# Sparse expert tiles routed through DRAM, stage by stage, in place of dense experts woven with the sampling convolution

## The chip, the core and the metric

One core of a Trainium2 chip runs one program. The metric is device time in microseconds. TensorE multiplies matrices (PE in the profile, PEld for its weight loads), VectorE is DVE, ScalarE is ACT, GpSimd is POOL, and SyncE (SP) issues most of the DMAs.

## The reference, cut to what matters

A batch of 8 images of 64 channels and 16x16 pixels goes through four residual blocks. A token is a pixel; there are 256 per image and 2048 in all.

```python
x = x + conv(ln_c(x))      # deformable sampling: 8 groups x 9 taps, bilinear, offsets from a depthwise conv; 2 products; SiLU
t = t + ffn0(ln_t(t))      # 8 experts, hidden 682: sum_e gates[n,e] * (silu(x w1_e) * (x w3_e)) w2_e ; gates: top 2 of 8
x = x + attention(ln_c(x)) # linear attention, 8 heads of 32: softmax(q), softmax(k), context = k v^T
t = t + ffn1(ln_t(t))      # 16 experts, hidden 128, same form, top 2 of 16
```

The reference computes every expert for every token and multiplies by gates, all but two of which are zero.

## The kernel before

Work is done image by image. The program has two streams of steps. `stream_a` of an image holds its layer norm, values, depthwise convolution, offsets, the sampling taps, the first residual and the routing of the first expert block. `stream_b` holds the experts of that block, attention, the second routing and the experts of the last block. A first walk does `stream_a` of image 0 while the expert weights are split into high and low parts (`piece`, L833). A loop of 7 rounds then weaves `stream_a` of image i with `stream_b` of image i-1, and a final walk does `stream_b` of image 7 alone. The order on each engine is written out by hand in `WEAVE`. Engines wait for each other through semaphores.

**Sampling.** A sampled value is a sum over 16 columns (a matrix product) and 16 rows (an elementwise product and a later sum). `columns` makes column distances on TensorE (L439, 2 groups of 128 partitions per tap), ScalarE turns them into weights (L693, L695), and `column_weights` stores them as high and low parts in `hx` (L898, L900). A unit is one tap k, one token tile t of 128 and one half h of the groups: two products of 512 columns (`bdh` L453, `bdl` L454), a multiplication by the row weights `hy` on VectorE out of PSUM (L914), and an addition into `acc` on GpSimd (L1084). There are 36 units per image, with two PSUM banks and two `prod` buffers. `hy` is made by L890 (DVE), L683, L687 (ACT) and L1075 (POOL). L921 sums the rows at the end.

**Experts.** Both blocks are dense: every expert runs over all 256 tokens of the image. A pair is two chunks of up to 128 hidden rows. `up` makes eight products of 256 columns (L523, L524, L537, L538), ScalarE applies SiLU (L752), VectorE multiplies (L985), and `down` adds two products into one bank (L548). There are 24 pairs for block 0 and 8 for block 1 in each image. The gate is applied beforehand: `gated` (L738, 4 scalings on ScalarE per two experts) makes a scaled copy of the input, `gate_unit` transposes (L503) and splits it (L745, L978). All weights stay in SBUF.

**Routing.** `top` finds the two largest logits, `gates` makes a row of gates for each token.

Layer norms take their inverse root on GpSimd (L1068, L1070).

Of the kernel before, what the change touches and what calls it, by code (L numbers as in the profile page):

```python
# [8 lines left out]
TT = PIX // P  # L29
G, GC, K = 8, 8, 9  # L30
GH = 4
NH = G // GH
E0, HID0, CH0 = 8, 682, 114
CPE0 = -(-HID0 // CH0)
E1, CH1 = 16, 128
NC0, NC1 = E0 * CPE0, E1
PAIRS0, PAIRS1 = NC0 // 2, NC1 // 2
PAIRS = PAIRS0 + PAIRS1
PPE0 = CPE0 // 2
UNITS = K * TT * NH  # L40
ADDS = UNITS - TT * NH
GU0, GU1 = E0 // 2, E1 // 2
SLOTS = 4
# [3 lines left out]
AUG = C + 4  # L47
STAGE = 1024
LAG = 2
RING = 6  # L50


def gating(m, first, end):

    out = []
    for u in range(first, end):
        out += [("gated", m, u)] + ([("gate_unit", m, u - 1)] if u > first else [])
    return out + [("gate_unit", m, end - 1)]

WEAVE = {
    "pe": """
        bbabbbbabb bbbbbabbbb bbbababbba bbbbbbbbbb bbbbabbaba abbaababba bbabaaaaba bababababa aabbabbaaa abaabaaaaa
        abaabaabbb abaabaabab bbabaababa bbabbbbbab ababa
        """,
    "act": """
        bbbabbbbab bbbbaabbba abbaabbaba bbbbbaabab bbbababbba bbabbbbbbb bbbbbbbbaa babbabaabb baaaaabaaa
        """,
    "dve": """  # L70
        babbabbbba bbaabababb baabbbbbba aaababbaab aabbaabaaa abbaaaabba baababaaba baabaabaaa aaabaabbab abababaaab
        bababaabab aabbababaa
        """,
    "pool": """
        aaaaabaaaa aaaaaaabaa aaaaaaaaaa aaaaaaaa
        """,
}


def stream_a():  # L80

    pre = [("x_tokens",), ("stats", 0), ("norm", 0), ("xn_channels",), ("cv1",), ("y",), ("values",)]
    pre += [("depthwise", r) for r in range(3)] + [("diagonal",), ("offsets",)]
    pre += [("row_distances", t) for t in range(TT)] + [("row_weights", t) for t in range(TT)]

    taps = [("columns", 0), ("column_weights", 0), ("columns", 1)]
    for k in range(K):
        units = [("tap" if k else "first_tap", k, q) for q in range(TT * NH)]
        taps += units[:1] + ([("column_weights", k + 1)] if k + 1 < K else [])
        taps += units[1:2] + ([("columns", k + 2)] if k + 2 < K else []) + units[2:]  # L90
    tail = [("sampled",), ("op",), ("cv2",), ("x1",), ("stats", 1), ("norm", 1), ("stack", 0), ("logits", 0), ("top", 0),
            ("exp", 0), ("gates", 0)]
    return pre + taps + tail + gating(0, 0, GU0)


def stream_b():

    def pairs(first, end, late=()):
        out = []
        for j in range(first, end):  # L100
            out += [("up", j)]
            out += (late[j - first] if j - first < len(late) else []) + ([("down", j - LAG)] if j >= first + LAG else [])
        return out + [("down", j) for j in range(end - LAG, end)]
    att = [("x2",), ("x2_tokens",), ("stats", 2), ("norm", 2), ("xn2_channels",), ("queries",), ("keys",),
           ("attn_values",), ("k_maxima",), ("q_maxima",), ("k_exp",), ("v_copy",), ("q_exp",), ("k_tokens",), ("context",),
           ("q_norm",), ("q_channels",), ("mix",), ("attend",), ("x3_tokens",), ("stats", 3), ("norm", 3), ("stack", 1),
           ("logits", 1), ("top", 1), ("exp", 1), ("gates", 1)]
    att += gating(1, 0, SLOTS)
# [42 lines left out]
def count(x):  # L151

    if isinstance(x, int):
        return x
# [1000 lines left out]
```

## Time and profile before

| | |
|---|---|
| runs, us | 1307.42, 1313.4, 1317.43; median 1313.4 |
| profiled execution, first to last instruction | 1318.4 us |
| PE, DVE, ACT, POOL busy | 1045.0, 849.9, 592.8, 395.3 us |
| mean granted TensorE clock | 0.813 of 2.4 GHz |
| DMA | 12.32 MB, mean 9 GB/s |

The profiled execution's own device time is not listed apart from its span. The span lies 0.4% above the median of the runs and inside 0.1% of the slowest of them, so nothing of size lies around it. Busy shares are averages over the first walk, seven rounds and the final walk.

### The profile page before, as it was taken

How to read it: one execution, taken by the hardware profiler on the slowest of the kernel's cores; microseconds unless marked ns; L12 is line 12 of the kernel's file. 1: busy time of each engine (PE TensorE's matmuls, PEld its weight loads, DVE VectorE, ACT ScalarE, POOL GpSimd, SP SyncE). 2: the span in 40 equal slices, each digit the busy share in tenths (PEclk: the TensorE clock that was granted, in tenths of full speed). 3: DMA queues.
4: the chain of work that ended last, by engine and by line, in shares of the span. 5: the costliest groups of instructions: out<-in, count | busy, mean ns of one | idle time of the engine just before them, and what ended most of it. 6: DMA issues, size and time to landing. Idle time of an engine off the chain costs nothing.

```text
span 1318.4 us, 17175 instructions
## 1 busy us (share of the span) xinstructions
PE 1045.0 (79%) x5184; PEld 712.9 (54%) x5184; DVE 849.9 (64%) x1608; ACT 592.8 (45%) x1261; POOL 395.3 (30%) x340
## 2 busy tenths in 40 slices
PE   2574697779887898778977798678976898779856
PEld 1341574546654675555745465455744575456534
DVE  2786567955587456964679556974688456974332
ACT  1422543563435634455435634455435624366343
POOL 0275015610265004630156103640157002650000
PEclk9955788778987778778887798888988779878956
DMA  4122000000000000000000000000000000000000
GB/s 129 53 67 66 19 1 1 1 3 3 0 0 0 5 0 0 0 2 3 0 0 0 4 1 0 0 2 3 0 0 0 4 0 0 0 0 3 0 1 2
DMA packets 5326, 12.32 MB, mean 9 GB/s; under 512 B 1118, under 2 KB 2342, under 8 KB 5094
## 3 DMA queue, kind: packets, MB, share of 16 engines
q1 hardware_dynamic: 4782, 9.02, 2.6%
q10 hardware_dynamic: 494, 2.81, 0.7%
q14 instruction: 40, 0.33, 0.1%
q8 instruction: 10, 0.16, 0.1%
HBM read 11.30 MB, written 0.52 MB: 9 GB/s over the span
## 4 chain that ended last, share of the span: by engine, by line
PE 54%; DVE 18%; issue 11%; ACT 8%; POOL 6%; DMA 1%; DVEq 0%; POOLq 0%; SPq 0%; ACTq 0%
PE ps_y L548 11%; PE ps_h L523 7%; POOL sb_acc L1084 5%; PE ps_h L537 5%; PE ps_h L524 4%; PE ps_h L538 4%; PE ps_t L453 4%; ACT sb_xg L738 4%; DVE sb_prod L914 3%; PE ps_m L439 3%; PE ps_t L454 3%; PE ps_t L421 3%; PE ps_h L503 2%; DVE sb_hx L898 2%; DVE sb_dsum L921 1%
## 5 line engine op out<-in xcount | busy, mean ns | idle before, releaser
L1084 POOL TENSOR_TENSOR sb_acc<-sb_acc,sb_prod 128x512 f32<-128x512 f32 x256 | 332.7, 1322 | 231.9 <-DVE sb_prod L914 230.6
L752 ACT ACTIVATE sb_hid<-ps_h 114x512 f32<-114x512 f32 (+1 forms) x256 | 149.8, 595 | 245.5 <-PE ps_h L524 245.0
L985 DVE TENSOR_TENSOR sb_hid<-ps_h,sb_hid 114x512 f32<-114x512 f32 (+1 forms) x256 | 171.8, 685 | 136.7 <-ACT sb_hid L752 104.0
L453 PE MATMUL ps_t<-sb_bdh,sb_hx 128*128 128x512 f32 x288 | 165.6, 575 | 62.8 <-DVE sb_prod L914 58.8
L914 DVE TENSOR_TENSOR sb_prod<-ps_t,sb_hy 128x512 f32<-128x512 f32 x256 | 172.1, 684 | 32.0 <-PE ps_t L454 17.1
L454 PE MATMUL ps_t<-sb_bdl,sb_hx 128*128 128x512 f32 x288 | 137.9, 479 | 0.0
L453 PEld LDWEIGHTS ps_t<-sb_bdh,sb_hx 128*128 128x128 f32 x288 | 66.5, 231 | 130.9 <-DVE sb_prod L914 103.4
L548 PE MATMUL ps_y<-sb_hid,sb_w2s 114*64 114x256 f32 x768 | 131.4, 426 | 0.0
L738 ACT ACTIVATE sb_xg<-sb_xn,sb_gt 128x128 f32<-128x128 f32 x384 | 120.1, 390 | 25.0 <-DVE sb_gt L973 25.0
L523 PE MATMUL ps_h<-sb_xh,sb_w1s 128*114 128x256 f32 x384 | 125.0, 345 | 0.0
L1068 POOL TENSOR_TENSOR sb_rs<-sb_mv,sb_epst 128x2 f32<-128x2 f32 x32 | 6.2, 195 | 375.1 <-DVE sb_mv L846 375.1
L537 PE MATMUL ps_h<-sb_xgh,sb_w3s 128*114 128x256 f32 x384 | 107.9, 300 | 9.6 <-DVE sb_hid L985 9.6
L1075 POOL TENSOR_TENSOR sb_hy<-sb_hy,sb_ym 128x1152 f32<-128x1152 f32 x16 | 34.2, 2155 | 263.4 <-ACT sb_hy L687 263.4
L439 PE MATMUL ps_m<-sb_dwT,sb_omx 68*128 68x256 f32 x288 | 99.8, 480 | 15.2 <-ACT sb_hat L693 13.8
L538 PE MATMUL ps_h<-sb_xgl,sb_w3s 128*114 128x256 f32 x384 | 106.6, 297 | 0.0
L524 PE MATMUL ps_h<-sb_xl,sb_w1s 128*114 128x256 f32 x384 | 106.0, 296 | 0.0
L523 PEld LDWEIGHTS ps_h<-sb_xh,sb_w1s 128*114 128x114 f32 x384 | 73.5, 191 | 57.2 <-ACT sb_hid L752 31.2
L693 ACT ACTIVATE sb_hat<-ps_m 128x512 f32<-128x512 f32 x72 | 42.8, 594 | 133.6 <-DVE sb_hx L900 127.3
L900 DVE SCALAR_TENSOR_TENSOR sb_hx<-sb_hx,sb_wide,sb_hat 128x512 fp32r<-128x512 f32 x72 | 96.7, 1343 | 2.5
L439 PEld LDWEIGHTS ps_m<-sb_dwT,sb_omx 68*128 68x128 f32 x288 | 65.9, 243 | 36.9 <-ACT sb_hat L693 17.7
L537 PEld LDWEIGHTS ps_h<-sb_xgh,sb_w3s 128*114 128x114 f32 x384 | 74.0, 193 | 11.3 <-DVE sb_hid L985 11.3
L524 PEld LDWEIGHTS ps_h<-sb_xl,sb_w1s 128*114 128x114 f32 x384 | 74.4, 194 | 1.4
(173 smaller groups left out, 1794.4 us busy)
## 6 DMA issues: line engine op xcount, KB each, us to landing
sb_hid<-in_w1T SPq DMA_DIRECT2D x16, 171.0 KB, 3.1
sb_hid<-in_w3T SPq DMA_DIRECT2D x16, 171.0 KB, 3.0
sb_w2s<-in_w2T ACTq DMA_DIRECT2D x1, 1368.0 KB
sb_hid<-in_u1T SPq DMA_DIRECT2D x4, 256.0 KB, 3.9
sb_hid<-in_u2T SPq DMA_DIRECT2D x4, 256.0 KB, 3.7
sb_omx<-in_omxT ACTq DMA_DIRECT2D x1, 612.0 KB
sb_xT<-in_x SPq DMA_DIRECT2D x8, 64.0 KB, 2.1
sb_u3s<-in_u3T ACTq DMA_DIRECT2D x1, 512.0 KB
```

Source lines behind the costliest of these rows:

```text
L439: last = mm(mb[:, h * PIX:(h + 1) * PIX], omx[:, o:o + P], dwT[:, :], start=True, stop=True)
L453: mm(tb[u % 2][:, :], w, bdh[:, h, :], start=True, stop=False)
L454: mm(tb[u % 2][:, :], w, bdl[:, h, :], start=False, stop=True).then_inc(s_pe_t, 1)
L523: mm(d, wa[:, o:o + ch], xh[m][:, :], start=True, stop=False)
L524: last = mm(d, wa[:, o:o + ch], xl[m][:, :], start=False, stop=True)
L537: mm(d, wb[:, o:o + ch], xgh[m][:, slot, x], start=True, stop=False)
L538: last = mm(d, wb[:, o:o + ch], xgl[m][:, slot, x], start=False, stop=True)
L548: last = mm(yb[c * C:(c + 1) * C, 0:PIX], w[0:ch, 2 * (j - first) + c, :], hid[0:ch, j % RING, c * PIX:(c + 1) * PIX], start=(j == first), ...
L738: last = af(xg[m][:, u % 2, t, e, :], xn[1 + 2 * m][:, t, :], ACT.Copy, scale=gt[m][:, t, 2 * u + e:2 * u + e + 1])
L914: v.tensor_tensor(o.rearrange("p (g c q) -> p g c q", g=GH, q=H), tb[u % 2][:, :].rearrange("p (g c q) -> p g c q", g=GH, q=H), w, ALU.mul ...
L985: v.tensor_tensor(hid[0:ch, j % RING, :], h3[j % 2][0:ch, :], hid[0:ch, j % RING, :], ALU.mult).then_inc(s_dve_hid, 1)
L1084: g.tensor_tensor(acc[:, t, h, :], acc[:, t, h, :], prod[:, u % 2, :], ALU.add).then_inc(s_pool_acc, 1)
```

## The change

The whole batch now goes through the blocks one after the other: `conv_order`, `moe0_order`, `attention_order`, `moe1_order`, `final_order`. Everything is unrolled; a step takes its place by a number, and an image's steps before and after its taps are spread over the taps of its neighbours.

**Sampling.** A unit is one tap and one token tile with all eight groups: four single products of 256 columns (K is 2 groups x 16 columns x 2 parts of the column weights x 2 parts of the values), 1024 elements for VectorE and for GpSimd. There are 18 units per image and three `prod` buffers. The column weights of three taps are made at once (128 x 768): ScalarE takes absolute value, ReLU and a high part, VectorE the low part, and SP copies these with 16 DMAs (32 partitions x 3 KB each) into the four partition groups of `hx`. The depthwise convolution is 9 products on TensorE, the second multiplication of `rows` is on VectorE, and the two output products become one (`opcv`).

**Experts.** Ranks of tokens within their experts are counted with products (`upper`, `ones`). `scatter` writes each normalized token to two rows of `xs` in DRAM. `route` makes tables of tiles on VectorE. Block 0 then runs 23 tiles (J0) of 256 rows with one expert each, 3 pairs per tile; block 1 runs 32 tiles (J1), two at a time. SP reads expert and row from the tables into registers and loads rows and weights of each tile from DRAM. Results go to `ys`; `gather` fetches two rows per token, and the gates are applied to them.

```diff
+        xs = nc.dram_tensor("xs", (E1 * CAP, C), f32).ap()
+        ys = nc.dram_tensor("ys", (J1 * TILE, C), f32).ap()
+            for g in range(E1):
+                sp.dma_start(xs[g * CAP:(g + 1) * CAP, :].rearrange("(p r) c -> p (r c)", p=P), zero[:, :]).then_inc(s_zero, 16)
...
+            def columns(n, r):                                     # SP
+                sp.wait_ge(s_act_hh, 2 * q + 2)
+                for part, src in ((0, hath[b]), (2, hath[b]), (1, hatl[b]), (3, hatl[b])):
+                    if part == 1:
+                        sp.wait_ge(s_dve_hl, q + 1)
+                    for j in range(NJ):
+                        sp.dma_start(hx[s][32 * part:32 * part + 32, j, :].bitcast(f32),
+                                     src[32 * j:32 * j + 32, :].bitcast(f32)).then_inc(s_hx[s], 16)
...
+            def load0(j):                                          # SP
+                e = sp.value_load(tab[0][0:1, 0, j:j + 1], min_val=0, max_val=E0 - 1)
+                r = sp.value_load(tab[0][0:1, 1, j:j + 1], min_val=0, max_val=E0 * CAP - TILE)
+                if j >= 2:
+                    sp.wait_ge(s_pe_mx, j - 1)
+                for d in range(2):
+                    sp.dma_start(xt[b][:, :, d, :], rows).then_inc(s_ldx[b], 16)
+                if j >= 2:
+                    sp.wait_ge(s_pe_dn, PAIRS * (j - 1))
+                sp.dma_start(w13[b][:, :].bitcast(f32), wsp[:, bass.ds(e * (2 * W0), 2 * W0)]).then_inc(s_ldw[b], 16)
+                sp.dma_start(w2[b][:, :], A["w2T"][:, bass.ds(e * (CPE0 * C), CPE0 * C)]).then_inc(s_ldw[b], 16)
...
+            def tap(n, k, t):                                      # TensorE
+                for j in range(NJ):
+                    last = mm(tb[u % 2][:, j * 256:(j + 1) * 256], hx[q % 3][:, j, o:o + P], vbd[n % 2][:, j * 256:(j + 1) * 256],
+                              start=True, stop=True)
...
+            def scatter(n, m):                                     # GpSimd
+                for t in range(TT):
+                    for z in range(2):
+                        g.indirect_dma_start(out=xs, out_offset=bass.IndirectOffsetOnAxis(ap=idx[m][:, TT * n + t, z:z + 1], axis=0),
+                                             in_=xr[m][n % 2][:, t, :], in_offset=None).then_inc(s_sc[m][n % 2], 16)
+            def gather(n, m):                                      # GpSimd
+                for t in range(TT):
+                    for z in range(2):
+                        g.indirect_dma_start(out=yg[b][:, t, z, :], out_offset=None, in_=ys[0:NJT[m] * TILE, :],
+                                             in_offset=bass.IndirectOffsetOnAxis(ap=jdx[m][:, TT * n + t, z:z + 1], axis=0))
```

`load1` (block 1, two tiles) makes four register reads and eight DMAs in the same way: four of rows (64 KB each), two of `u12` (128 KB), two of `u3` (32 KB). `split_out` writes the split weights of both blocks to `wsp` and `usp` in DRAM.

## Rows read from the trace of the kernel before

**Rows 1.** The page's first part: engine, busy us and share, instructions.

```profile
PE 1045.0 (79%) x5184; PEld 712.9 (54%) x5184; DVE 849.9 (64%) x1608; ACT 592.8 (45%) x1261; POOL 395.3 (30%) x340
```

**Rows 2.** The page's chain of waits, its shares by engine.

```profile
PE 54%; DVE 18%; issue 11%; ACT 8%; POOL 6%; DMA 1%; DVEq 0%; POOLq 0%; SPq 0%; ACTq 0%
```

**Rows 3.** The timeline of SP's queue: image loads of two successive rounds.

```profile
274.90 0.49 SPq L376 DMA_DIRECT2D sb_xT<-in_x  x1
...
428.53 0.49 SPq L376 DMA_DIRECT2D sb_xT<-in_x  x1
```

**Rows 4.** Busy time by window: stretch, length, busy of PE, PEld, DVE, ACT, POOL, clock, DMA.

```profile
0.00:19.60 19.60, 0.00 (x0) 0.00 (x0) 1.28 (x7) 0.00 (x0) 0.20 (x4) 1.00 0.59 153
60.00:118.00 58.00, 38.83 (x78) 22.00 (x78) 47.42 (x54) 14.12 (x22) 42.15 (x31) 0.54 0.25 68
200.00:360.00 160.00, 134.01 (x676) 91.31 (x675) 106.22 (x204) 74.42 (x159) 50.32 (x43) 0.83 0.01 1
1203.50:1244.50 41.00, 41.00 (x292) 28.73 (x292) 17.90 (x26) 15.36 (x26) 0.00 (x0) 1.00 0.01 3
1244.50:1276.50 32.00, 15.30 (x49) 10.54 (x48) 11.53 (x44) 7.23 (x20) 1.76 (x4) 0.57 0.00 1
1276.50:1318.40 41.90, 29.07 (x128) 20.40 (x128) 11.91 (x19) 20.40 (x50) 0.00 (x0) 0.62 0.01 2
```

**Rows 5.** Groups of instructions: busy us, mean ns; idle before and its releaser.

```profile
L914 DVE TENSOR_TENSOR sb_prod<-ps_t,sb_hy 128x512 f32<-128x512 f32 x256 | 172.1, 684 | 32.0 <-PE ps_t L454 17.1 <-POOL sb_acc L1084 13.5
...
L738 ACT ACTIVATE sb_xg<-sb_xn,sb_gt 128x128 f32<-128x128 f32 x384 | 120.1, 390 | 25.0 <-DVE sb_gt L973 25.0
L752 ACT ACTIVATE sb_hid<-ps_h 114x512 f32<-114x512 f32 x192 | 112.3, 594 | 182.1 <-PE ps_h L524 181.8
...
L439 PE MATMUL ps_m<-sb_dwT,sb_omx 68*128 68x256 f32 x288 | 99.8, 480 | 15.2 <-ACT sb_hat L693 13.8 <-ACT sb_ym L679 1.4
...
L1075 POOL TENSOR_TENSOR sb_hy<-sb_hy,sb_ym 128x1152 f32<-128x1152 f32 x16 | 34.2, 2155 | 263.4 <-ACT sb_hy L687 263.4
...
L1070 POOL TENSOR_TENSOR sb_rs<-sb_rs,sb_mhalf 128x2 f32<-128x2 f32 x32 | 22.3, 697 | 2.5
...
L890 DVE TENSOR_TENSOR sb_hy<-sb_ym,sb_wide 128x1152 f32<-128x1152 f32 x16 | 20.9, 1350 | 0.0
...
L921 DVE TENSOR_REDUCE sb_dsum<-sb_acc 128x64 f32<-128x1024 f32 x16 | 18.7, 1209 | 1.7 <-POOL sb_acc L1084 1.7
...
L886 DVE TENSOR_TENSOR sb_bdl<-sb_acc,sb_bdh 128x1024 fp32r<-128x1024 f32 x8 | 9.8, 1226 | 11.3 <-ACT sb_bdh L675 11.3
...
L1068 POOL TENSOR_TENSOR sb_rs<-sb_mv,sb_epst 128x2 f32<-128x2 f32 x32 | 6.2, 195 | 375.1 <-DVE sb_mv L846 375.1
```

**Rows 6.** Single lines: durations in ns as min/median/max, first and last start.

```profile
L1084 POOL TENSOR_TENSOR sb_acc<-sb_acc,sb_prod x256: 1257/1281/1906, 58.6 to 1173.7; 128x512 f32<-128x512 f32 x128
```
```profile
L900 DVE SCALAR_TENSOR_TENSOR sb_hx<-sb_hx,sb_wide,sb_hat x72: 750/1634/1654, 50.1 to 1162.5; 128x512 fp32r<-128x512 f32 x72
```
```profile
L833 DVE SCALAR_TENSOR_TENSOR sb_w1s<-sb_xgh,sb_wide,sb_hid x8: 916/925/2167, 26.7 to 68.9; 128x684 fp32r<-128x684 f32 x8
```
```profile
L371 SPq DMA_DIRECT2D sb_hid<-in_w1T x16: 465/597/828, 3.1 to 58.4; - x16
```

**Rows 7.** DMA queue, and issues with KB each and median us to landing.

```profile
q1 hardware_dynamic: 4782, 9.02, 2.6%
```
```profile
sb_hid<-in_w1T SPq DMA_DIRECT2D x16, 171.0 KB, 3.1
...
sb_xT<-in_x SPq DMA_DIRECT2D x8, 64.0 KB, 2.1
```

More of the change, by code:

```diff
@@ L47, with spread, conv_order @@
 AUG = C + 4
+UNITS = K * TT
+ADDS = UNITS - TT
+TRI = 3
+NTRI = K // TRI
+RING = 4
+W0 = CPE0 * CH0
 STAGE = 1024
-LAG = 2
-RING = 6
-def gating(m, first, end):
+def spread(steps, start, end):
+    return [(start + (end - start) * (i + 0.5) / len(steps), s) for i, s in enumerate(steps)]
+def conv_order(n_pieces):
     out = []
[L56 to L77, printed above, removed]
@@ L80, in stream_a @@
[L80 to L93, printed above, removed]
@@ L96, in stream_b @@
[L96 to L108, printed above, removed]
-    late = [[]] + [[("gated", 1, u), ("gate_unit", 1, u)] for u in range(SLOTS, GU1)]
-    return pairs(0, PAIRS0) + att + pairs(PAIRS0, PAIRS, late) + [("x4",)]
@@ L644, in _ @@
+            pe.wait_ge(s_const, n_const)
+            pe.wait_ge(s_set, 4)
+            mm(pb[0:C, 0:C], op_[:, :], cv2[:, :], start=True, stop=True).then_inc(s_pe_comb, 1)
+            for name, *args in order:
+                if name in steps:
+                    steps[name](*args)
         @block.scalar
@@ L797, in walk @@
[L797 to L805 removed]
+                    af(ex[m][:, t, :], lg[m][:, t, :], ACT.Exp, bias=nm[m][:, t:t + 1], accum_out=sm[m][:, t:t + 1])
@@ L808, in _ @@
+            for name, *args in order:
+                if name in steps:
+                    steps[name](*args)
         @block.vector
@@ L1047, in walk @@
-            def walk(order, images):
-                for stream, name, *args in order:
-                    if name in steps:
-                        steps[name](images[stream], *args)
-            walk(first, {"a": 0, "w": 0})
-            with dve.Fori(1, B) as i:
-                walk(steady_order(WEAVE["dve"], steps), {"a": Image(i, 0), "b": Image(i, -1)})
-            walk(final, {"b": B - 1})
+                b = n % 2
+                dve.wait_ge(s_pe_mm, n + 1)
+                dve.wait_ge(s_dve_qn, 5 * n + 5)
@@ L1058, in _ @@
+            for name, *args in order:
+                if name in steps:
+                    steps[name](*args)
         @block.gpsimd
@@ L1086, in _ @@
-            steps = {"stats": rsqrt, "row_weights": row_weights, "tap": tap}
-            def walk(order, images):
-                for stream, name, *args in order:
-                    if name in steps:
-                        steps[name](images[stream], *args)
-            walk(first, {"a": 0, "w": 0})
-            with pool.Fori(1, B) as i:
-                walk(steady_order(WEAVE["pool"], steps), {"a": Image(i, 0), "b": Image(i, -1)})
-            walk(final, {"b": B - 1})
+            pool.wait_ge(s_set, 4)
@@ new lines, in stats0, with stats1, combine, stats3 @@
+            def stats0(n):
+                rsqrt(n, 0)
+            def stats1(n):
+                rsqrt(n, 1)
+            def combine(n):
+                rsqrt(n, 2)
+            def stats3(n):
+                rsqrt(n, 3)
+            steps = {"stats0": stats0, "stats1": stats1, "combine": combine, "stats3": stats3, "tap": tap, "scatter": scatter, "mout": mout, "gather": gather, "nout": nout}
+            for name, *args in order:
+                if name in steps:
+                    steps[name](*args)
```

1629 lines of the change are left out of this document (968 added, 661 removed).

## The prediction

> **What bounds the kernel now.** Read the busy shares first [rows 1]: TensorE has 79% of the span, VectorE 64%, and no engine is full. The chain of waits [rows 2] gives TensorE 54% and VectorE 18%, so the end is set by TensorE work and by handovers. The windows [rows 4] split that. In a round (200 to 360) TensorE is busy 134 of 160 us at a clock of 0.83, VectorE 106. The rounds follow each other at 153.6 us (274.90 to 428.53 [rows 3]). The final walk shows what `stream_b` costs alone: 41.0 us for the 24 pairs of block 0, with TensorE full at clock 1.00 (2.4 GHz), or 1.71 us per pair; 32.0 us for attention and the second routing, a bare chain in which TensorE is busy 15.3 us at 0.57, near the lower level of 1.2 GHz; and 41.9 us for block 1. So dense experts are about a third to a half of the work, sampling most of the rest. The first walk (60 to 118) shows sampling without experts: GpSimd busy 42.15 of 58 us, VectorE 47.42, and TensorE at 0.54 is not the limit. That stretch matters most, because the change makes sampling a stage of its own.
>
> **The change, part by part.** The sum is made against the span of 1318.4 us and scaled by 1313.4/1318.4 at the end. Stages no longer overlap, so their times add.
>
> *Start.* TensorE begins at 19.6 us today, when the constants have landed [rows 4]. After, 16 fills of 512 KB (8.4 MB) stand on SP's queue before the first copies into `hx`. SP's queue moved 9.02 MB in 2.6% of 16 engines' 1318.4 us, 548 engine-us, so 263 GB/s with all 16 busy [rows 7]. The fills take 32 us, constants and images before them 5 to 10, and the copies another few: the first tap at 48 us. If the fills were free it would be about 42, at half the rate 75.
>
> *Sampling, per image.* Four parts:
> - TensorE halves its columns, from 72 x 512 to 72 x 256. It was not the limit in the first walk and gains nothing here.
> - GpSimd adds 16 x 1024 elements. No row has this shape. Half the elements take 1257 ns at least [rows 6], 1152 elements of another product 2155 [rows 5]. Twice the first is 2.51 us, the line through both shapes gives 1.98. I take 2.32, twice 1257 less the 195 ns that a two-element addition costs [rows 5], since that keeps the same operation: 37.1 us.
> - VectorE's taps go from 36 x 0.684 to 18 x 1.22 us (1024 elements at L886's 1226 [rows 5]), 22 us. Operations with two SBUF inputs are three low parts of 768 elements (0.95 each by the same rows), four of 1152 for the row weights (1.35), one of 1024 (1.28), and the split of weights, 20 pieces over 8 images (2.5 us an image at 916 ns for 684 elements [rows 6]): 12.1 us. Sums of rows are 2 x 1.21. With layer norms, top-2 and ranks, some 7 us of small ones, VectorE has about 43.
> - L900 takes 750 ns alone and 1634 in the median, while GpSimd's addition goes from 1257 to 1906 [rows 6]. The two seem to exclude each other. So the additions and the 12.1 us are added: 49.2. GpSimd also has two inverse roots (0.9 each) and four indirect DMAs for the scatter, 5.2 us, in all 56.2.
>
> In the first walk's stretch GpSimd's busy time and the free-standing durations of VectorE's two-input work fill nearly all 58 us; I divide by 0.96: 58.5. Three places drain the ring. At the image border no addition runs while VectorE sums rows and multiplies twice (5 us), since tap 0 has no addition. At each of two layer norms VectorE waits for GpSimd and then restarts it (2.2 us each). That gives 68 us per image, 544 for 8. The bounds are 58 (no drain visible) and 75.
>
> The Trainium skill (SBUF — State Buffer, Who interferes with whom) says that VectorE with two SBUF inputs and GpSimd reading SBUF exclude each other for whole instructions. The trace agrees, 750 against 1634 ns. Without that rule an image would cost the larger of 43 and 44 plus drains, about 54, and the sum would be 112 us lower; with it, the 1024-wide addition holds VectorE off for up to 2.3 us at a time.
>
> *Indirect DMAs* (32 for each of two scatters and two gathers). No row shows one. Nearest below is SP's issue, 0.53 us, above it GpSimd's 2.16 us instruction [rows 5, 6]. I take 1.3 of GpSimd's time each, the middle, and 2.1 us to landing as for the small load [rows 7].
>
> *From the last tap to the first expert product.* Nothing overlaps: sums, two products, SiLU, residual, norm, logits, top-2, ranks are 20 to 23 us by the 32 us chain of attention, whose second half holds the same steps. Four scatters, landing, two register reads and the first 0.9 MB of weights add 18. I take 41.
>
> *Block 0.* 69 pairs stand in place of 192. A tile is 3 x 1.71 + 0.6 us for its transposes, 5.7 at full clock. Its weights (896 KB) may load only when the tile two before is done. From issue to landing that is 0.5 + 3.4 (896 KB at 263 GB/s) + 1.9 = 5.8 us. A buffer is in use 6.0 us at 2.4 GHz, 7.2 at the rounds' 0.83. Two buffers give (7.2 + 5.8)/2 = 6.5 us per tile, 150 for 23. Bounds: 125 (TensorE alone) and 220 (clock at its lower level, as in the 0.54 stretch). The gating (L738's 120 us of ScalarE) goes; it was beside other work but not in the final walk.
>
> *Attention.* Into it 13 us (last tile out, gather, landing). The lone chain was 32.0 us; ranks make it 35. Two images are in flight, 17.5 each if they matched. GpSimd must issue 8 indirect DMAs (10.4 us) and their landing between one image's ranks and the next combination but one, where some 7 us are free: 5 us more. I take 23 each, 8 x 23 + 15 = 199. Bounds are 150 and 255. The clock will be low: the same steps ran at 0.57.
>
> *Block 1.* Into it 18 us, as before block 0. TensorE needs about 2.8 us per two tiles at 2.4 GHz, 5 at 1.2. SP issues 8 DMAs at 0.53 and makes 4 register reads from SBUF. No row has a register read; it lies between nothing and the 2.1 us of a small load's landing. I take 0.8, near the issue. 4.2 + 3.2 = 7.4 us, so SP is the bound: 16 x 7.4 = 118. Bounds are 80 and 200.
>
> *End.* Store landing 3, 32 gathers at 1.3 = 42, last tokens out 7: 52.
>
> **Sum:** 48 + 544 + 41 + 150 + 13 + 199 + 18 + 118 + 52 = 1183 us; times 0.9962 is 1178.
>
> **Rivals.**
> *Handovers hide better.* Sampling at 58 an image (-80), attention at 18 (-40), block 0 at 125 (-25), block 1 at 80 (-38): 1000. For it: VectorE and GpSimd have three buffers now, not two. Against: in no window of before did an engine stay full but TensorE in the pure expert walk.
>
> *Indirect DMAs cost GpSimd 2.2 us, not 1.3.* Sampling +29, attention +58, end +29, transitions +11: 1310, scaled 1305. It becomes no change at that price. Nothing in the trace speaks against it, as GpSimd issues no DMA at all now. The Trainium skill (DMA: Bandwidth & Descriptors, Specifications) gives GpSimd's path about 1 us to the first byte; by it the sum would be some 30 us lower. No run here shows it.
>
> *The copies into `hx` set the pace (slower than before).* Three taps' weights are ordered five of six units ahead, 5 x 68/18 = 18.9 us. The way there is three products (L439), three ScalarE passes of some 0.85 us by L752's 594 for 512, a low part (0.95), together 5.6 us, then 16 issues on SP's queue and 2.1 to land [rows 5, 7]. At 0.53 us an issue this is 16.2, just hidden. From 0.70 us it decides, and at 1.2, with 8.0 us of stall in each of 24 triples, it gives 1183 + 192, scaled 1370. L371 takes 465 to 828 ns [rows 6], so the threshold lies inside the spread that one line shows; but its median is 597, and SP had little else. SP also issues each split's three DMAs in that order.
>
> That the change doesn't cut the work is excluded: J0 and J1 are fixed tile counts, and 69 pairs and 32 tiles are issued whatever the routing.
>
> **How the numbers follow.** The forecast as summed has 0.48, with its own range of 1070 to 1270. The fast rival has 0.18, costly indirect DMAs 0.18, the copies 0.16. A measurement of this kernel tells about 1% from no change, so 1300 to 1327 is "same". The forecast and the fast case are faster, the indirect case is split between faster (0.09) and same or worse, the copies are slower. Faster 0.76, same 0.07, slower 0.17. The range leaves out half of the fast case's low side and most of the copies' case beyond 1370: 990 to 1370. Of single terms the sampling stage carries the widest money, 8 x (58 to 75).
>
> **What the profile after would show.** Right: five stages in the slices; in sampling, GpSimd busy two thirds or more with additions near 2.3 us, VectorE's low parts stretched beyond 0.95, little waiting for `hx`; block 0 at 6 to 7 us per tile with TensorE waiting for weight DMAs; attention at 23 us an image, clock near 0.5; SP's queue dense in block 1. Wrong: TensorE waiting in sampling for `hx` (copies), GpSimd's queue filled by indirect DMAs, additions of 2.0 us or of more than 2.6, or a clock at 1.2 GHz through block 0.

## The result and the profile after

The changed kernel takes 1373.2 us (median of 4, 1369.0 to 1374.5) against 1310.5 for the kernel before beside it: a ratio of 1.047, 95% interval 1.042 to 1.052. It is slower. The forecast was 1178 us and faster, with a range up to 1370, so the sign was wrong. The profiled execution has a span of 1370.3 us.

The page's first part, as [rows 1] of before:

```profile
PE 749.1 (55%) x3080; PEld 556.4 (41%) x3080; DVE 603.9 (44%) x1158; ACT 331.9 (24%) x605; POOL 518.1 (38%) x379
```

Every engine but GpSimd lost work, TensorE 296 us and VectorE 246. No engine now has more than 55% of a longer span, so the time was lost in waits. That GpSimd is busy 51% of the sampling stage, where the forecast named two thirds or more as the sign of being right, is the first hint. The windows cut at the stages (columns as in [rows 4]; start, sampling, tail and routing, block 0, attention, routing, block 1, end) say where:

```profile
0.00:56.00 56.00, 21.44 (x68) 14.66 (x68) 14.74 (x37) 14.63 (x18) 1.10 (x6) 1.00 0.58 203
56.00:762.00 706.00, 372.50 (x1274) 285.29 (x1274) 381.39 (x475) 182.25 (x264) 362.81 (x184) 0.92 0.30 75
762.00:790.00 28.00, 6.41 (x22) 3.94 (x22) 11.04 (x50) 7.06 (x15) 4.82 (x6) 0.50 0.15 44
790.00:956.00 166.00, 143.13 (x964) 101.91 (x964) 63.80 (x114) 58.49 (x114) 16.37 (x23) 0.94 0.49 146
956.00:1203.00 247.00, 128.33 (x448) 102.78 (x448) 92.72 (x393) 41.57 (x137) 78.84 (x96) 0.50 0.04 9
1203.00:1211.00 8.00, 0.00 (x0) 0.00 (x0) 3.44 (x11) 0.00 (x0) 0.96 (x1) 0.50 0.18 42
1211.00:1318.00 107.00, 71.38 (x286) 46.08 (x286) 28.51 (x47) 24.50 (x48) 20.24 (x29) 0.60 0.40 104
1318.00:1370.30 52.30, 5.90 (x20) 1.76 (x18) 8.27 (x33) 3.40 (x9) 32.92 (x36) 0.50 0.16 35
```

Against the forecast: start 56 (48), sampling 706 (544), tail 28 (41), block 0 166 (150), attention with the way into it 247 (212), routing 8 (18), block 1 107 (118), end 52.3 (52). Sampling is off by 162 us and attention by 35; the rest cancels. In sampling VectorE and GpSimd are each busy about half of the time. The waits of that stretch, by engine and releaser (total us, times, longest us):

```profile
POOL sb_acc L1310 <- DVE sb_prod L1044: 366.5, 72, 63.5
DVE sb_stage_w L983 <- ACT sb_stage_h L761: 101.3, 15, 14.1
DVE sb_hats L1030 <- ACT sb_hats L814: 55.0, 22, 3.9
ACT sb_stage_h L761 <- DMA sb_stage<-in_w1T: 49.4, 7, 13.9
ACT sb_stage_h L761 <- DMA sb_stage<-in_w3T: 47.8, 6, 14.3
DVE sb_prod L1044 <- PE ps_t L504: 35.5, 28, 6.3
DVE sb_hy L1022 <- ACT sb_hy L800: 33.9, 14, 2.4
DVE sb_vbd L1011 <- ACT sb_vh L783: 33.5, 7, 6.0
DVE sb_xn L997 <- POOL sb_rs L1362: 20.0, 7, 2.9
```

L1030 makes the low part of the column weights, L1022 is the last multiplication of the row weights, L1011 lays out the values for the products, L997 is the last operation of a layer norm.

Read it from the top. GpSimd, whose additions were to be the larger part of the bound, waits 366 us for VectorE's products, 63.5 of them before its first addition. Between its first addition and its last (80.8 to 761.1 us) GpSimd is idle for 317 us. In 187 of them VectorE works, 96 on products of taps and 91 on its other instructions; in the other 131 both stand. VectorE's own waits are mostly within its steps, for ScalarE or GpSimd to do the middle of them. The largest in total is at the split of the weights (L983), and ScalarE in turn waits there for a load.

The spacing of the row sums (L1052) gives the time of an image. They start at 165.0, 268.4, 371.5, 463.3, 544.3, 625.4, 704.0 and 761.1 us: 103 us for images 1 and 2, with five weight pieces in each spacing, 92 for image 3 with four, 81.1 for images 4 and 5 without pieces, 78.6 for image 6, which took 81.1 in the other kernels with the same sampling, and 57 for the last, which prepares no successor. The forecast had 68 for all.

### The profile page after: what moved, and what is told of

Its sections match the earlier page's. It is cut to its first block and busy times, and to the rows that moved or that the text cites. A ratio compares the mean times of both kernels' runs of the same rounds, so it can differ in the third digit from the quotient of the medians.

```text
span 1370.3 us, 10821 instructions
## 1 busy us (share of the span) xinstructions
PE 749.1 (55%) x3080; PEld 556.4 (41%) x3080; DVE 603.9 (44%) x1158; ACT 331.9 (24%) x605; POOL 518.1 (38%) x379
## 5 line engine op out<-in xcount | busy, mean ns | idle before, releaser
L1310 POOL TENSOR_TENSOR sb_acc<-sb_acc,sb_prod 128x1024 f32<-128x1024 f32 x128 | 307.3, 2417 | 366.6 <-DVE sb_prod L1044 366.5
L504 PE MATMUL ps_t<-sb_vbd,sb_hx 128*128 128x256 f32 x576 | 171.6, 454 | 179.8 <-DVE sb_prod L1044 148.0
L504 PEld LDWEIGHTS ps_t<-sb_vbd,sb_hx 128*128 128x128 f32 x576 | 134.7, 321 | 216.9 <-DVE sb_prod L1044 161.5
L1044 DVE TENSOR_TENSOR sb_prod<-ps_t,sb_hy 128x1024 f32<-128x1024 f32 x128 | 153.5, 1218 | 43.8 <-PE ps_t L504 35.5
L1322 POOL DMA_INDIRECT xs<-sb_xr,sb_idx x64 | 81.7, 1276 | 105.1 <-DVE sb_idx L1121 89.3
L983 DVE SCALAR_TENSOR_TENSOR sb_stage_w<-sb_stage_h,sb_wide,sb_stage 128x684 fp32r<-128x684 f32 (+1 forms) x20 | 27.4, 1372 | 101.3 <-ACT sb_stage_h L761 101.3
L1345 POOL DMA_INDIRECT sb_prod<-ys,sb_jdx x64 | 61.3, 958 | 23.0 <-issue 20.9
L1030 DVE TENSOR_TENSOR sb_hats<-sb_hat,sb_hats 128x768 fp32r<-128x768 f32 x24 | 36.6, 1526 | 66.2 <-ACT sb_hats L814 66.2
L490 PE MATMUL ps_c<-sb_dwT,sb_omx 68*128 68x256 f32 x144 | 65.0, 623 | 0.0
L474 PE MATMUL ps_pa<-sb_ypad,sb_diag 64*64 64x256 f32 x144 | 63.5, 634 | 0.0
L865 ACT ACTIVATE sb_stage<-ps_t 114x512 f32<-114x512 f32 x69 | 41.2, 597 | 70.3 <-PE ps_t L572 68.5
L468 PE MATMUL ps_c<-sb_vp,sb_yrep 65*128 65x64 f32 x256 | 53.9, 409 | 2.5 <-ACT sb_yrep L771 2.4
L468 PEld LDWEIGHTS ps_c<-sb_vp,sb_yrep 65*128 65x128 f32 x256 | 53.3, 321 | 3.6 <-ACT sb_yrep L771 3.2
L571 PE MATMUL ps_t<-sb_hx,sb_hats 128*114 128x256 f32 x138 | 44.2, 340 | 12.2 <-DMA sb_acc<-in_w2T 11.7
L1022 DVE TENSOR_TENSOR sb_hy<-sb_hy,sb_ym 128x1152 f32<-128x1152 f32 x16 | 30.6, 1911 | 38.8 <-ACT sb_hy L800 38.8
```

The lines of the kernel that those rows point to most:

```text
L468: last = mm(cb[:, r * C:(r + 1) * C], yrep[:, r * P:(r + 1) * P], vp[:, :], start=True, stop=True)
L474: last = mm(pa[0:C, 0:PIX], diag[:, k, :], ypad[:, k // 3:k // 3 + H, k % 3:k % 3 + W], start=(k == 0), stop=(k == K - 1))
L490: last = mm(cb[:, i * PIX:(i + 1) * PIX], omx[:, k * P:(k + 1) * P], dwT[n % 2][:, :], start=True, stop=True)
L504: last = mm(tb[u % 2][:, j * 256:(j + 1) * 256], hx[q % 3][:, j, o:o + P], vbd[n % 2][:, j * 256:(j + 1) * 256], start=True, stop=True)
L571: mm(d, w13[b][:, o:o + CH0], xh[b][:, :], start=True, stop=False)
L865: af(hid[q % RING][0:CH0, :], h1[q % 2][0:CH0, :], ACT.Silu).then_inc(s_act_s, 1)
```

## The experiments

Two theories of the stage. *O, order:* VectorE runs its steps in program order, and the middle of a step on another engine leaves it standing while GpSimd has nothing to add. *X, exclusion:* GpSimd's additions and VectorE's instructions with SBUF operands alone can't run together, and their sum is the bound. Beside them stood *C*, the rival of the prediction, the copies into `hx`. For attention: *G*, a chain through GpSimd's order, against *K*, TensorE's low clock and the hops.

The medians (us), each with the kernel before on the same chip; "image" is the spacing of row sums of an image without pieces, "last sum" the start of the last pair of row sums in the profile:

```
kernel                            time    before   ratio (95%)             image  last sum
changed                           1373.2  1310.5   1.047 (1.042-1.052)     81.1   761.1
loads early                       1317.5  1310.0   1.005 (1.001-1.010)     81.1   705.6
no split                          1286.5  1310.0   0.982 (0.973-0.991)     81.1   673.6
VectorE in two phases             1307.7  1310.0   1.001 (0.997-1.004)     75.7   696.9
no additions                      1310.1  1310.0   0.998 (0.995-1.001)     72.2   699.1
gathers ahead                     1333.0  1317.3   1.014 (1.005-1.022)     81.1   764.1
loads early and two phases        1299.3  1317.3   0.988 (0.979-0.998)     75.8   687.6
three engines, gathers ahead      1231.7  1317.3   0.937 (0.928-0.945)     72.0   662.5
half copies                       1378.5  1317.3   1.048 (1.039-1.057)     81.0   767.3
chain later, combine ahead        1207.6  1310.2   0.924 (0.919-0.930)     74.4   650.1
units of 512                      1352.5  1310.2   1.034 (1.027-1.041)     76.3   737.7
all orders, units of 512          1200.6  1312.0   0.912 (0.905-0.919)     70.3   643.5
three engines, no additions       1159.1  1312.0   0.881 (0.871-0.890)     64.4   587.8
```

The kernel before took 1310.0, 1317.3, 1310.2 and 1312.0 us beside them, on four chips. So where rows of different chips lie within some 10 us of each other, their ratios are to be compared, not their times. Four kernels leave work out and only price it: no split (the weights stay unsplit), the two without additions, and half copies.

### The pieces of weights

Loads early:

```diff
+    out += [(0.05 + 0.2 * i - 0.12, ("piece_high", i)) for i in range(n_pieces)]
 # SP, in piece(j), behind the write of piece j - 1:
-                load(j)
+                load(j + 1)
 # ScalarE takes its part at piece_high, VectorE at piece
```

> Each piece's two loads are issued one piece earlier (on SP, behind the write of the piece before), and ScalarE makes its high part 0.12 of an image ahead of VectorE's low part; nothing else moves. Theory O (order: VectorE, whose program order holds the low part, the hats, the rows and the additions' products, stands in a wait while GpSimd has nothing to add): the 20 low parts of L983 waited 101 + 15 + 14 us in all, and most of that goes: sampling 706 -> 610 to 640 us, the total 1373 -> about 1290, all of it in images 0 to 3 (103 -> 84 us each). Rival C (SP's queue of 16 copies for each group of three taps sets the pace): the same transfers stand in the same queue, so at most 10 to 20 us go. Rival X (GpSimd's additions and VectorE's SBUF-only instructions can't run at the same time, and their sum is the bound): 20 low parts of 1.3 us each remain in the sum, so 103 stays near 95, total about 1340.

Measured: 56 us less. Images 1 and 2 take 87 and 90 us instead of 103, image 3 90. L983's wait has left the head of VectorE's list. Sampling ends 56 us earlier where O had named 66 to 96; C had at most 20 and X some 33 for the total, so O is nearest, and too high.

No split:

```diff
-            steps = {"piece": piece, ...          (ScalarE and VectorE)
 # SP: wsp and usp are written from stage as it was loaded
```

> The split of the weights into a high and a low part is left out: the pieces are loaded and written back as they are, and neither ScalarE nor VectorE touches them (so the products of block 0 and block 1 take unsplit weights; times of these stages are the same). It prices all that the pieces cost the two engines. Theory O: images 0 to 3 take what images 4 to 6 take, 81 us instead of 103: total 1373 - 90 = about 1283, and close to the run with the loads issued earlier (within 30 us of it). Rival C: the 60 transfers of the pieces remain, so under 30 us go. Rival X: 20 x 1.3 us of SBUF-only work go, with their waits remaining elsewhere: about 1340.

Measured: 87 us less, and all images from 1 to 6 take 81.1 us. So the pieces cost 87 us in all, of which the late loads, with ScalarE's part standing directly before VectorE's, were 56. The forecast had charged VectorE's own time for them, 2.5 us an image, 20 in all. The 31 us that stay with early loads are close to the 27.4 us for which L983 is busy in the changed kernel (20 instances, 921 to 3177 ns: some are held by additions).

### VectorE in two phases

```diff
+LATE = ("rows", "columns", "values", "stats0", "stats1", "top", "piece")
+    out += [(t + 0.07, (s[0] + "_late", *s[1:])) for t, s in out if s[0] in LATE]
 # VectorE, in rows: the subtraction stays at "rows",
 # the wait for ScalarE and the multiplication stand at "rows_late", the others alike
```

> VectorE's second halves, those that wait for ScalarE, GpSimd or SP within a step (rows' multiplication, the low part of the hats, the values' block form, the norms' last operation, the gates, the low part of a piece), stand 0.07 of an image (one or two taps) later in VectorE's order; the other engines' orders stay, and no work is added or removed. Theory O: of VectorE's 325 us of idle time in sampling the waits inside steps (of the order of 250 us with the pieces') are filled with taps: images 4 to 6 fall from 81 to 62-68 us, images 0 to 3 from 103 to 75-85; total about 1220 to 1260. Rival X: GpSimd's 16 additions (37.6 us) and VectorE's SBUF-only instructions (some 18 us) follow one another, with 8 us of GpSimd's other work: not under 64 us an image, and likely 72; total about 1300. Rival L (the chain of ten steps that prepares the next image sets the period, through ScalarE and TensorE): the late halves lengthen this chain, so the time stays or grows: 1370 to 1420.

Measured: 66 us less, an image 81.1 -> 75.7. L falls. The direction is O's, but it had named 113 to 153 us in all and 13 to 19 an image. The total of about 1300 was X's figure, so this run alone doesn't part O from X; the next does. Windows of one image without pieces, of the changed kernel first, then of this one:

```profile
546.60:627.70 81.10, 50.20 (x170) 38.40 (x170) 46.90 (x63) 23.09 (x34) 47.15 (x24) 1.00 0.26 61
```

```profile
488.30:564.00 75.70, 50.14 (x170) 38.24 (x170) 53.02 (x63) 23.21 (x34) 47.74 (x24) 1.00 0.27 63
```

VectorE idles 22.7 us instead of 34.2, but the same 63 instructions take 6.1 us longer: more of them now meet an addition. The largest part is the two last operations of a layer norm, in the changed kernel and in this one:

```profile
562.80 0.54 DVE L997 TENSOR_SCALAR sb_xr<-sb_x1t,sb_mv,sb_rs 128x64 f32<-128x64 f32 x2 [2.86 <-POOL sb_rs L1362]
```

```profile
502.33 4.63 DVE L1003 TENSOR_SCALAR sb_xr<-sb_x1t,sb_mv,sb_rs 128x64 f32<-128x64 f32 x2
```

What is left of the waits in this image is mostly for TensorE:

```profile
DVE sb_prod L1057 <- PE ps_t L506: 16.0, 6, 6.7
DVE sb_dsum L1065 <- POOL sb_acc L1330: 2.3, 1, 2.3
```

TensorE issues 16 and 9 products of the next image in one go, and it stands in its own order for the sums and norms of the image before.

### No additions

```diff
-g.tensor_tensor(acc[n % 2][:, t, :], acc[n % 2][:, t, :], prod[a % 3][:, :], ALU.add)
+g.tensor_tensor(acc[n % 2][:, t, 0:8], acc[n % 2][:, t, 0:8], prod[a % 3][:, 0:8], ALU.add)
```

> GpSimd adds 8 columns of the 1024 of each tap instead of all (so the sampled sums lack the rest); everything else, the waits too, stays. Theory O: GpSimd isn't the bound, it is starved: only the instructions of VectorE that were held to the end of an addition, and the taps that found the ring full (8 us), get shorter: 6 to 12 us an image, total 1373 - 50 to 100 = 1275 to 1325, and an image without pieces takes 70 us or more. Rival X (GpSimd's additions, alone or with VectorE's SBUF-only work, are the bound): an image without pieces falls to VectorE's 45 to 50 us, total about 1100.

Measured: 63 us less, an image 72.2. GpSimd is busy 10.8 us of it. So GpSimd's additions are no bound (X in its strong form falls: it said 45 to 50), but they cost 9 us an image by what they do to VectorE. The row weights' multiplication (L1022), durations in ns as min/median/max, with the additions and without:

```profile
L1022 DVE TENSOR_TENSOR sb_hy<-sb_hy,sb_ym x16: 1357/1359/4305, 49.3 to 690.0; 128x1152 f32<-128x1152 f32 x16
L1077 DVE TENSOR_SCALAR sb_nm<-sb_mx x16: 168/170/2264, 208.9 to 1194.8; 128x2 f32<-128x2 f32 x16
```

```profile
L1022 DVE TENSOR_TENSOR sb_hy<-sb_hy,sb_ym x16: 1357/1359/1368, 49.5 to 647.7; 128x1152 f32<-128x1152 f32 x16
L1077 DVE TENSOR_SCALAR sb_nm<-sb_mx x16: 168/169/170, 206.2 to 1131.8; 128x2 f32<-128x2 f32 x16
```

Without additions no instance is stretched. An image has VectorE busy 37.9 us instead of 46.9, and that 9.0 us is the whole gain of 8.9. The product of a tap, which reads PSUM, isn't held at all:

```profile
L1044 DVE TENSOR_TENSOR sb_prod<-ps_t,sb_hy x128: 1206/1217/1226, 79.5 to 754.3; 128x1024 f32<-128x1024 f32 x128
L1310 POOL TENSOR_TENSOR sb_acc<-sb_acc,sb_prod x128: 2327/2352/3473, 80.8 to 758.8; 128x1024 f32<-128x1024 f32 x128
```

### The copies

```diff
-sp.dma_start(hx[s][32 * part:32 * part + 32, j, :], src[32 * j:32 * j + 32, :])
+sp.dma_start(hx[s][32 * part:32 * part + 32, j, 0:384], src[32 * j:32 * j + 32, 0:384])
```

> Each of the 384 copies into the taps' operand takes half of the 768 columns (the other half is zeroed once, so its taps are left out of the sums); the number of transfers stays. Theory O: the first copy alone had TensorE waiting, so the time stays within 15 us of 1373. Rival C (the copies' transfer time sets the pace of the taps): an image takes 8 us less or more, total about 1300.

Measured: 1378.5, a ratio of 1.048 against the changed kernel's 1.047: no difference. The copies' transfer time costs nothing. Their number was not varied; that it costs little too rests on the changed kernel's trace, where TensorE waits for a copy once:

```profile
  PE ps_t L504: 14.4, 1
```

### Both edits of VectorE's order, then TensorE's order too

> Both edits of sampling together: the pieces' loads one piece earlier with ScalarE ahead of VectorE (alone it gave 56 us), and VectorE's second halves 0.07 of an image later (alone 66 us, in which VectorE still waited 64 us for pieces). If both are waits of VectorE's order, they add up in most: images 0 to 3 fall to 80, images 4 to 6 stay at 75.7: total 1265 to 1285. If TensorE's order is by now what holds the period (in the two-phase run VectorE waited 16 of 75.7 us for it), the sum is less: images 0 to 3 stay at 85 or more, total 1290 to 1300.

Measured: 1299.3. By the ratios to the kernel before, that is some 17 us better than two phases alone and 23 better than early loads alone, where the two had given 66 and 56. The gains don't add: images 1 to 3 stay at 89 to 91 us. That is the second of the two expectations: in this kernel VectorE waits 93.5 us for TensorE's products between 100 and 640 us, about as in the run with two phases alone (89.7 us). That images with pieces gain so little is not explained further.

```diff
+# TensorE: values in 8 + 8 products, depthwise in 3 + 3 + 3, taps between them
+        out += [(n - 0.6, ("values_first", n)), (n - 0.52, ("depthwise_first", n, 0)),
+                (n - 0.47, ("depthwise_first", n, 1)), (n - 0.41, ("depthwise", n)), (n - 0.355, ("offsets", n))]
-        out += spread([("sampled", n), ("z", n), ("x1", n), ...], n + 1.02, n + 1.75)
+        out += [(n + 1.1, ("sampled", n)), (n + 1.16, ("sampled_next", n)), (n + 1.215, ("z", n)), ...]
+# "_next" is the place of TensorE's and ScalarE's part
```

> The edits of the two runs before, and also TensorE's side of sampling: the 16 products of the values and the 9 of the depthwise step stand in two and three parts between taps, and of the chain that follows the taps (sums, z, x1, norm, logits, ranks) each engine's step stands one tap behind that of the engine that it waits for; with the gathers ahead in attention. No work is added. Theory O, now for two engines: an image of sampling falls from 75.7 to 64-70 us (TensorE busy 50, VectorE 53, GpSimd 48), in all 8 images, sampling 706 -> about 570, attention to about 165: total 1373 - 136 - 80 = about 1155, between 1130 and 1200. Rival X (VectorE's SBUF-only work and the additions exclude one another, 9 us of an image by the run without additions): more overlap lengthens VectorE further, an image stays at 72 to 76: total about 1200 to 1230.

Measured: 1231.7 us, 6.3% faster than the kernel before. An image falls to 72.0 and the total to 1231.7. The first is the low end of X's 72 to 76, the second just past its 1200 to 1230; neither is in O's 64 to 70 and 1130 to 1200. X's mechanism is not seen, though: VectorE is busy 53.7 of 72.0, against 53.0 in the two-phase run, so there is hardly any further lengthening:

```profile
462.80:534.80 72.00, 50.75 (x172) 37.86 (x171) 53.74 (x63) 23.32 (x34) 47.02 (x24) 1.00 0.29 69
```

### What holds the rest

> The kernel of the run with three engines and the gathers, with GpSimd adding 8 columns of 1024 (the sampled sums lack the rest). In the changed kernel this took 9 us off an image of 81, all of it time by which VectorE's SBUF-only instructions had been held. With the waits inside VectorE's steps gone, theory X' (the additions and the holding are by now the larger part of what is above TensorE's 50 us) gives an image of 72 -> 58 to 62 us: total 1232 - 85 = about 1145. Rival P' (TensorE's order and VectorE's wait for its products, 14 to 16 us an image, is the larger part): 72 -> 64 to 67, total 1170 to 1185.

Measured: an image takes 64.4 us, a gain of 7.6 of 72.0 by the additions; P' named 64 to 67, and for the total 1170 to 1185. Measured were 1159.1, between that and the 1145 of X'. VectorE's busy time is 37.8. Between 100 and 600 us it waits, above all, for this:

```profile
DVE sb_prod L1074 <- PE ps_t L523: 174.3, 53, 14.7
```

So nearly without additions the stage would still take 14 us an image more than TensorE's 50.

> One part of the change alone is undone: the changed kernel's taps are taken in two units of 512 columns (products' release, VectorE's multiplication, GpSimd's addition, with the waits between them per half), all else as changed. Theory O: the size of the unit isn't what is slow; the halves cost VectorE 36 x 0.15 us/2 and GpSimd 0.16 us a tap more, under 3 us an image each, and a held instruction of VectorE waits for half as long: total 1373 within -20 and +25 us. Rival U (the large unit, with 2 in PSUM and 3 in the ring in place of finer ones, is what starves GpSimd): an image of 81 us falls to 72 or less: total 1300 or less.

```diff
 # tap(n, k, t), on TensorE, VectorE and GpSimd:
+for h in range(2):
+    c = slice(512 * h, 512 * h + 512)
     ... the same operation on [:, c], with a release and a wait of its own
```

Measured: 1352.5, 21 us less than the changed kernel (1.034 against 1.047 in the ratio), at the edge of what O allowed. The halves cost GpSimd 2.6 us of busy time an image more, and the image still takes 76.3 instead of 81.1. VectorE's busy time falls from 46.9 to 43.6: it is held for shorter additions (the small operation that took up to 2.26 us behind one now takes at most 1.09). The large unit was thus a loss of its own here, of about a third of the 63 us by which the change was slower.

> From the run with three engines' orders and the gathers, two further moves of order. In sampling the chain behind the taps (sums to scatter) stands 0.35 of an image later, out of the stretch in which TensorE also prepares the next image. In attention the combine step with its norm stands ahead of the ranks of the image two before (0.5n - 0.1 instead of + 0.075). Theory P (TensorE's crowded stretch, in which VectorE waited 14 of 72 us an image for its products, is what is left beside the exclusion): an image 72 -> 64 to 68 us, images with pieces 86 -> 78 to 82, sampling -35 to -50 us; attention's period 23.0 -> 18 to 20 us, -25 us; total 1232 -> 1155 to 1175. Rival X (GpSimd and VectorE exclude one another on SBUF operands, and a fuller overlap lengthens VectorE's instructions in its place): an image stays at 70 to 73 us, VectorE's busy time rises over 55 us; total about 1200. Rival K for attention (TensorE's 15 us of busy time at the clock of 0.50 and its order): the period stays at 21 to 23 us.

```diff
-out += [(n + 1.1, ("sampled", n)), ... (n + 1.76, ("scatter", n, 0))]
+out += [(n + 1.45, ("sampled", n)), ... (n + 2.11, ("scatter", n, 0))]
+out += [(0.5 * n - 0.1, ("combine", n))]      # attention, was at 0.5 * n + 0.075
```

Measured: 1207.6. P falls: an image takes 74.4 us, not 64 to 68. X's reading doesn't hold either, as VectorE's busy time falls to 49.7. Moving the chain out of the crowded stretch puts TensorE's waits elsewhere (39 us for the norm, 34 for the top-2, 25 for the next image's norm between 90 and 600 us). Still the stage ends 12 us earlier. The row sums stand a third of an image later here, so their spacings cover other pieces; counted from first tap to first tap, images 1 to 3 take 79, 80 and 83 us where they took 86, 86 and 89, a gain of 18, and images 4 to 6 lose 7. Why the images with pieces gain from the move stays open. Attention's period falls to 21.6, in K's range of 21 to 23 and not in the 18 to 20 of the other reading.

> The orders of the run with three engines (the chain behind the taps at its place there, not 0.35 later), the gathers and the combine step ahead in attention, and the taps in units of 512 columns as in the run that undid the units alone. If the units' gain (4.8 us an image there: 81.1 to 76.3) comes from shorter holds and waits between the three engines, it remains in part beside the mended orders: an image 72 -> 67 to 70 us, sampling -15 to -35 us against the run with three engines, attention 21.6 us an image: total 1180 to 1200. If the units' gain was the same waits that the orders have since removed, an image stays at 72 or rises by the 2.6 us of GpSimd's extra time: total 1205 to 1230.

Measured: 1200.6 us, 8.8% faster than the kernel before and the best of those that leave nothing out. An image takes 70.3 us, 0.3 above the first theory's range: 1.7 of the 4.8 us of the smaller unit remain beside the mended orders, so most of that gain was the same waits. Sampling ends 19 us before that of the run with three engines.

### Attention

In the changed kernel one image follows another at 30.2 us (first scatters at 1059.76 and 1089.94). The chain of waits between them, start, length, what (those through GpSimd):

```profile
1058.87 0.14 DVE sb_pick L1116
...
1059.76 1.06 POOL xs L1322
...
1063.66 1.44 POOL xs L1322
...
1065.40 1.00 POOL sb_prod L1345
...
1067.97 0.95 POOL sb_prod L1345
...
1069.23 2.37 DMA sb_prod<-ys,sb_jdx
1071.60 0.02 issue
1071.62 0.49 DVE sb_x2b L1181 x2
```

From the ranks of image n-2 to the combination of image n lie four scatters, four gathers and their landing, 11.8 us. The gathers depend on nothing in that chain; only GpSimd's order puts them behind.

```diff
-        out += spread([("gather", n, 0), ("combine", n), ...
+        out += [(0.5 * n - 0.26, ("gather", n, 0))]
```

> In the attention stage the four gathers of image n stand ahead of the four scatters of image n-2 in GpSimd's order (at 0.5n - 0.26 instead of 0.5n + 0.025); no work is changed. Theory G (the period of 30.2 us an image is a chain through GpSimd's order: rank, 4 scatters 5.3 us, 4 gathers 5.2 us, landing 2.4 us, then the norm): combine no longer waits for 12 to 13 us of this, so a period is 18 to 21 us, the stage 247 -> 150 to 175, total 1373 - 70 to 95 = about 1290. Rival K (TensorE at half its clock and the hops between the engines set the period, and the wait for the gather only covers another): the period stays over 27 us, total 1350 or more.

Measured: the period falls to 23.0 us (scatters at 1050.31 and 1073.38) and the total by 40 us. G's mechanism is shown, its size isn't: it had named a period of 18 to 21 us and a total of about 1290 (measured 1333.0), and of the 11.8 us, 7.2 went. VectorE's waits in the stage, of the changed kernel and of this one:

```profile
DVE sb_x2b L1181 <- DMA sb_prod<-ys,sb_jdx: 52.1, 7, 9.4
DVE sb_hy L1231 <- PE ps_c L645: 23.1, 8, 3.8
```

```profile
DVE sb_hy L1232 <- PE ps_c L646: 23.1, 8, 3.8
DVE sb_x2b L1182 <- DMA sb_prod<-ys,sb_jdx: 9.4, 1, 9.4
```

The wait for the gather is gone but for the first image. The next in the chain is the combine step behind the context product of the image before, in VectorE's order. With the combine step ahead of it the period is 21.6 us (the run with the chain later), of which TensorE is busy 16 (128 us for 8 images in the windows above). K is not excluded for this rest.

## Why the prediction was wrong

- *Sampling per image, "Three places drain the ring ... That gives 68 us per image": this step failed.* The durations of single instructions were right, and additions do hold VectorE. But the sum of the two, 49.2 us of GpSimd's and VectorE's work one behind the other, was not what set the pace: with the additions all but gone an image still took 72.2 us, more than the 68 forecast with them. What set it, besides the hold, were waits in the engines' orders, and the list of drains had few of them. It named one border and two norms (9.4 us). It left out VectorE's waits inside the column weights, the row weights, the values' layout and the gates, and TensorE's long steps. An image without pieces measured 81.1. By single edits, 9 us of it are the additions' hold on VectorE, which the 49.2 us of the sum had meant to cover; 5.4 VectorE's order, 3.7 more TensorE's, 4.8 the size of the unit. These overlap, and even without additions and with mended orders 64.4 remain. VectorE's waits could have been listed from the code before the run: each of these steps has ScalarE or GpSimd between two VectorE instructions, and nothing between them in VectorE's order.
- *The split of weights, "20 pieces over 8 images (2.5 us an image ...)": the second mis-sized term.* Counted as VectorE's busy time, 20 us, it cost 87. A step that three engines and a queue share costs the wait for the slowest hand, and the load was issued only at its turn, behind 16 copies. The prediction saw the queue ("SP also issues each split's three DMAs in that order") and gave it no price.
- *"For it: VectorE and GpSimd have three buffers now."* VectorE found the ring full for 8 us in all of sampling. A longer ring does nothing for an engine that waits for its input.
- *The additions at 2.32 us, taps at 1.22 us:* 2.35 in the median and 1.22. Right.
- *Indirect DMAs, 1.3 us of GpSimd each, 2.1 to land:* in the mean 1.28 of busy time for a scatter (954 to 2141 ns; 1.48 in sampling, 1.08 in attention) and 0.96 for a gather, with 0.30 of issue between two, landing 2.2 and 2.4. Right, and the rival with 2.2 us is excluded. The prediction's "some 30 us lower" at 1.0 us is 38 by its own count of 128.
- *The rival with the copies, 1370 us:* it named the measured time, by a mechanism that didn't occur. An issue took 592 ns in the median, below its threshold of 0.70; half the bytes changed nothing. (Its three terms before the issues, 1.4, 2.6 and 0.95, give 4.9 us and not 5.6; with that the threshold is 0.74.)
- *Attention, "5 us more. I take 23 each": this failed too.* 30.2. The mechanism was named there, GpSimd's 8 indirect DMAs between ranks and combination, but set against "some 7 us" that weren't free: the stretch lies on the chain in full length, 11.8 us. That the period with the gathers ahead is 23.0, as taken, is chance: the 23 was for the other order.
- *Block 0 at 6.5 us a tile:* 7.2 at a clock of 0.94. TensorE was busy 143.1 of 166 us, 6.2 a tile, where 5.7 was taken at full clock. Part of that is the clock: at 0.98 in the two-phase run the same 964 products took 137.4 us, 6.0 a tile. Waits of 11.7 us for weights and 11.1 for ScalarE's copy of a finished tile came on top; the second had no term. *Block 1, 118:* 107, with SP waiting 0.2 us in all, so it was the bound as forecast, at a smaller price: *register reads at 0.8 us* were 0.45 (276, 152 and 18 ns of three instructions). *Start, 48:* 56; a fill landed in 6.5 us. *Tail, 41:* 28, and the routing before block 1 8 of 18. *End, 52:* 52.3. The errors of the stages other than sampling and attention cancel to 10 us; that is luck.
- *The stages add:* held. Before, TensorE was busy 134 of 160 us in a round, with the experts' products beside sampling; now it is busy 373 of 706 in sampling, and nothing else is there to fill its waits. That this is the deeper cause is argued from these two windows; no run wove experts and the new sampling together.

## What to carry to other kernels

When work that overlapped is split into stages, the price of a stage isn't the busiest engine's time. Walk its program order on each engine and add, for each step that passes through another engine and back, the whole way there, unless independent work stands between. Then mend it by placing each engine's part of a step one unit behind that of the engine it waits for, loads first: orders alone took this kernel from 4.7% slower than the kernel before to 7.6% faster, orders with the smaller unit to 8.8%. None of the kernels that leave nothing out reached the forecast 1178. Mended waits don't add up, so measure after each one what is late next.

## What the runs showed of the hardware, unexpected

VectorE's smallest operations are held by a GpSimd addition as well: one on 128x2 elements, with a single SBUF input (L1077 above), took 0.17 us alone and 2.26 behind an addition. The sums of rows, with one input of 1024 elements, were not held. In the changed kernel none of them meets an addition; with the chain later 12 of the 16 run wholly or nearly so beside one:

```profile
L1082 DVE TENSOR_REDUCE sb_dsum<-sb_acc x16: 1203/1210/1220, 158.1 to 651.2; 128x64 f32<-128x1024 f32 x16
```

The Trainium skill (SBUF — State Buffer, Who interferes with whom) names copies, casts and `tensor_scalar` as operations that can contend with GpSimd for the shared ports, under conditions on their operands, and `tensor_reduce` as one that never does on this chip. These rows agree.

One instruction can be held for several additions. The row weights' multiplication, 1.36 us alone, took 6.62 us in the kernel with three engines' orders while GpSimd ran three additions without a gap. The timelines of VectorE and GpSimd there:

```profile
524.59 6.62 DVE L1052 TENSOR_TENSOR sb_hy<-sb_hy,sb_ym 128x1152 f32<-128x1152 f32 x1 [0.16 <-ACT sb_hy L819]
```

```profile
523.01 6.98 POOL L1347 TENSOR_TENSOR sb_acc<-sb_acc,sb_prod 128x1024 f32<-128x1024 f32 x3
```

VectorE begins 1.6 us into the first and ends 1.2 us after the third. So the better GpSimd is fed, the longer a hold can last. (The 6.1 us of the two-phase run came otherwise: more small instructions were held, each behind one addition.)

TensorE's granted clock made no difference in an image of sampling. Windows of one image without pieces, of the kernel without the split and of the kernel with the gathers ahead, which have the same program there:

```profile
373.10:454.20 81.10, 50.19 (x170) 38.41 (x170) 46.90 (x63) 23.11 (x34) 47.15 (x24) 0.50 0.26 61
```

```profile
625.80:706.90 81.10, 50.20 (x170) 38.44 (x170) 46.89 (x64) 23.11 (x34) 47.14 (x24) 1.00 0.26 60
```

At a granted clock of 0.50 (1.2 GHz) and of 1.00 (2.4 GHz) TensorE's 170 products were busy for the same 50.2 us. A tap's four products took 1.22 us in both; what sets that pace wasn't tested. A low clock in the page isn't by itself a cost. In block 0 it seems to be one: the same 964 products were busy 143.1 us at 0.94 in the changed kernel and 137.4 at 0.98 in the two-phase run.
